# Four sequence layers on one core: three residual additions moved from VectorE to TensorE and ScalarE, new instruction orders, and a set-up that loads on two queues

## What is computed

```python
def attention_layer(x):                 # L0 and L3: linear attention, L1: softmax attention with 16 heads
    xn = layernorm(x) * w + b
    q, k, v = xn @ Wq + bq, xn @ Wk + bk, (xn @ Wv + bv) * mask
    y = attention(q, k, v)              # L0, L3: softmax of q and of k, then y = q (k^T v)
    h = layernorm(y) * (1 + scale(cond)) + shift(cond)
    return x + silu(h) @ Wout + bout    # the residual addition

def state_space_layer(x):               # L2
    s = modulated(layernorm(x)); u = layernorm(s)
    z1, z2 = (scan of width 16 over the 256 rows, forwards and backwards, for 512 channels each)
    return x + gate * ((silu(mx) * (z1 + z2)) @ Wf + bf + s)

x = L0(x); x = L1(x); x = L2(x); x = L3(x)
```

## Time and profile before

| | us |
|---|---|
| median of 3 runs | 4430.05 (4429.83 to 4433.16) |
| the profiled execution | 4430.37 |
| its span, first to last instruction | 4428.6 |
| from the start to the first scan product on POOL | 302.6 |
| from there to the last one's end | 4068 |
| from there to the last instruction | 57 |

### The profile page before, as it was taken

How to read it: one execution, slowest core, us unless ns; L and a number is a source line. 1 busy time by engine, 2 the same in 40 slices (tenths; PEclk the granted TensorE clock), 3 DMA queues, 4 the chain that set the end, 5 groups by cost and what they waited for, 6 DMA issues and landing times.

```text
span 4428.6 us, 74058 instructions
## 1 busy us (share of the span) xinstructions
PE 3722.4 (84%) x26464; PEld 2478.3 (56%) x26464; DVE 4050.2 (91%) x5619; ACT 3609.1 (81%) x8678; POOL 3849.4 (87%) x1772
## 2 busy tenths in 40 slices
PE   5988888889888888888888888888888888888664
PEld 3665555556565555555555555555655555556432
DVE  4449999989999999999999999999999999999995
ACT  0368878878988899889888998898888988988763
POOL 0019988989999999999999999999999999999994
PEclk6899999989999999999999999999999999999876
DMA  4033444543444445434444444344444444444541
GB/s 122 11 75 91 94 105 95 118 113 82 117 117 114 109 113 120 111 91 112 117 117 112 110 117 117 91 106 117 117 114 107 117 117 103 94 117 114 123 107 32
DMA packets 334160, 462.12 MB, mean 104 GB/s; under 512 B 56204, under 2 KB 165847, under 8 KB 333789
## 3 DMA queue, kind: packets, MB, share of 16 engines
q1 hardware_dynamic: 333632, 457.32, 43.7%
q10 hardware_dynamic: 158, 0.08, 0.0%
HBM read 370.26 MB, written 86.50 MB: 103 GB/s over the span
## 4 chain that ended last, share of the span: by engine, by line
ACT 28%; DVE 18%; PE 18%; POOL 7%; issue 5%; DMA 2%; SPq 0%; POOLq 0%; ACTq 0%; DVEq 0%
ACT ps L706 11%; PE ps L171 10%; DVE ps L721 5%; POOL S_X L767 5%; ACT A_ring L472 3%; DVE A_sm L429 3%; DVE S_X L721 3%; PE ps L804 3%; DVE S_X L736 2%; POOL S_X L780 2%; PE ps L376 2%; ACT C_xh L154 1%; PE ps L545 1%; ACT T_v L303 1%; DVE C_dd L579 1%
## 5 line engine op out<-in xcount | busy, mean ns | idle before, releaser
L767 POOL TENSOR_TENSOR S_X<-S_slot,S_bc 128x1024 f32<-128x1024 f32 x1024 | 2403.2, 2366 | 174.8 <-PE ps L804 119.2
L706 ACT ACTIVATE ps<-S_slot,acol 128x256 f32<-128x256 f32 x4096 | 1742.7, 468 | 190.5 <-DVE S_X L736 180.8
L721 DVE TENSOR_TENSOR_SCAN ps<-ps,S_X 128x512 f32<-128x512 f32 x1088 | 1300.0, 1214 | 37.4 <-POOL S_X L767 19.6
L780 POOL TENSOR_TENSOR S_X<-S_X,S_bc 128x1024 f32<-128x1024 f32 x480 | 1132.6, 2366 | 38.7 <-DVE S_X L721 32.6
L721 DVE TENSOR_TENSOR_SCAN S_X<-ps,S_X 128x512 f32<-128x512 f32 x960 | 1141.2, 1208 | 16.3 <-ACT ps L706 13.7
L736 DVE TENSOR_TENSOR S_X<-ps,S_bc 128x512 f32<-128x512 f32 x1088 | 712.5, 675 | 5.7 <-issue 0.2
L804 PE MATMUL ps<-S_X,sum 128*32 128x256 f32 x8192 | 615.6, 403 | 102.6 <-POOL S_X L780 62.4
L804 PEld LDWEIGHTS ps<-S_X,sum 128*32 128x32 f32 x8192 | 198.9, 112 | 388.8 <-issue 169.2
L429 DVE TENSOR_REDUCE A_sm<-ps 128x4 f32<-128x1024 f32 x256 | 311.0, 1215 | 62.7 <-PE ps L376 59.5
L376 PE MATMUL ps<-A_kP,A_qP 32*128 32x256 f32 x2048 | 292.7, 403 | 45.5 <-DVE A_sm L429 31.4
L395 PE MATMUL ps<-A_qP,A_kP 32*128 32x256 f32 x2048 | 296.7, 407 | 21.6 <-ACT A_ring L472 15.2
(11 more groups left out here) (295 smaller groups left out, 6882.0 us busy)
## 6 DMA issues: line engine op xcount, KB each, us to landing
S_slot<-scr_dd SPq DMA_DIRECT2D x1024, 256.0 KB, 4.7
scr_dd<-C_dd SPq DMA_DIRECT2D x64, 1024.0 KB, 5.3
S_bc<-scr_bc SPq DMA_DIRECT2D x256, 256.0 KB, 6.3
L_xin<-in_x SPq DMA_DIRECT2D x32, 256.0 KB
scr_x<-A_x SPq DMA_DIRECT2D x32, 256.0 KB, 5.8
T_x<-scr_x SPq DMA_DIRECT2D x32, 256.0 KB
out_x<-xs SPq DMA_DIRECT2D x32, 256.0 KB, 6.1
T_gate<-scr_gate SPq DMA_DIRECT2D x32, 128.0 KB
```

What stands on the lines that cost most here:

```text
L706: ins = a.activation(B["bank"][half_at(b, u, i)][:, n * T:(n + 1) * T], B["slot"][:, s, j, 0, :], ACT.Exp, scale=K.k["acol"][:, s, LINES * ...
L721: v.tensor_tensor_scan(line(x if u in ON_POOL else decay), line(decay), line(x), 0.0, ALU.mult, ALU.add).then_inc(S.scan.sem, 1)
L767: g.tensor_tensor(B["X"][:, u % RING], B["slot"][:, s, :, 1, :], rep(B["bc"][:, s, q, :], 1, LINES), ALU.mult).then_inc(S.b.sem, 1)
L780: g.tensor_tensor(B["X"][:, u % RING], B["X"][:, u % RING], rep(B["bc"][:, s, NQ + q, :], 1, LINES), ALU.mult).then_inc(S.cp.sem, 1)
```

## The change

**The additions.** `dve_film` is gone. `project` takes the old x as one more product, identity times x, in float32, which adds it to h in PSUM: two more products of 128x256 for each layer and batch. A step at the end of `act_film` copies the sum from PSUM to where the new x belongs, and carries the waits that the addition had. Who waited for the addition now waits for this copy.

**Loads of L0.** The input of a batch gets a semaphore of its own (`xin`), so that VectorE starts the norm's statistics with it; the mask row and the columns `L_pc` are waited for only by TensorE ahead of its k product.

**Orders.** All strings of `FIRST` and `TURN` are new. The rounds hold the same steps, but for the three additions on VectorE and the three copies on ACT.

**Set-up.** SP no longer waits ahead of its loads. 16 of them (masks, conditions, the weights of the conditioned norms) are issued by ACT. The scaling of the projections moves from VectorE to ACT. VectorE sets `bias` and splits the mask while the loads run. The bias row's way through DRAM moves from ACT to SP, behind all of its loads. The block no longer waits for the stored `pcol` to land; the loads that need it wait. The memsets of the main block, but for `A_vA`, move ahead into the set-up, and no engine but VectorE waits at the start of the main block.

```diff
-FILM_DVE = ["ystat0", "ystat1", "ymv0", "ymv1", "x"]
-FILM_ACT = ["ynm", "yln", "yrs", "ynb0", "ynb1", "yn0", "yn1", "h0", "h1", "sig1", "sig2", "sig3"]
+FILM_DVE = ["ystat0", "ystat1", "ymv0", "ymv1"]
+FILM_ACT = ["ynm", "yln", "yrs", "ynb0", "ynb1", "yn0", "yn1", "h0", "h1", "sig1", "sig2", "sig3", "x"]
...
-def project(p, bank, xT, w, bias, ones, c):
+def project(p, bank, xT, w, bias, ones, c, ident=None, x=None):
     for t in range(TT):
-        ins = matmuls(p, bank[:, t * D:(t + 1) * D], [(xT[:, k, t * P:(t + 1) * P], w[:, k, :]) for k in range(KD)] + [(ones[:, 0:P], bias)])
+        plus = [] if x is None else [(ident[:], x[:, t, :])]
+        ins = matmuls(p, bank[:, t * D:(t + 1) * D], [(xT[:, k, t * P:(t + 1) * P], w[:, k, :]) for k in range(KD)] + [(ones[:, 0:P], bias)] + plus)
...
     p.wait_ge(S.dve.sem, S.dve.at(b, "qsub"))
+    if L == "L0":
+        p.wait_ge(K.land["a"].sem, K.land["a"].at(b))
...
-    v.tensor_tensor(flat(x_out[:]), bank["o"][:, 0:512], flat(x[:]), ALU.add).then_inc(S.dve.sem, 1)
...
+    yield
+    a.wait_ge(S.pe.sem, S.pe.at(b, "o"))
+    if L == "L0" and b >= 2:
+        a.wait_ge(K.S["C"].act.sem, K.S["C"].act.at(b - 2, "xn1"))
+        a.wait_ge(K.land["x_out"].sem, K.land["x_out"].at(b - 2))
+    a.activation(flat(x_out[:]), bank["o"][:, 0:512], ACT.Copy).then_inc(S.act.sem, 1)
...
-LOADS = {"attention": 31, "conditions": 21, "scans": 21}
+LOADS = {"attention": 31, "masks": 3, "conditions": 13, "ada": 5, "scans": 21}
...
-                q.wait_ge(vector, 12)
...
-            q.dma_start(scr["pcol"].rearrange("b p n -> p b n"), M["pcol"][:]).then_inc(stored, 16)
-            q.wait_ge(stored, 16 * 3)
+            q.dma_start(scr["pcol"].rearrange("b p n -> p b n"), M["pcol"]).then_inc(K.W.columns, 16)
+            q.wait_ge(stored, 16 * 2)
...
-    "Pool": "SSCPSSSSSSSPPPSSSCSPSPSSPSPSSSPSTSPPSSSPSASPSPSCSPSLS",
+    "Pool": "SSSSTCPPSSPSPSSPSSSPSPSSPSASPSPSSCPLSSSSPSSSPSSSCPPSS",
```

More of the change, by code:

```diff
@@ L413, in pe_softmax @@
     ins.then_inc(S.pe.sem, 1)
[L414 removed]
+    yield from pe_film(p, K, S, B["ke"], B["xT"], {n: bank[i] for n, i in BANKS[L].items()}, L, b, B["x"][:, b % 2])
 def dve_softmax(v, K, b):
@@ L1214, in _ @@
             t = InTurn(a, scalar)
-            a.preload_act_table_set(ACT_SET)
+            with nc.allow_non_contiguous_dma(reason="columns of bias vectors, once"):
+                load(a, "masks", M["mi"][:], W["mask_BxS_ik0"])
+                load(a, "masks", M["mf"][:, 1, :], W["mask_BxS_ff1"])
+                load(a, "masks", M["mf"][:, 2, :], W["mask_BxSx1_fk1"].rearrange("b t a -> b (t a)"))
+                load(a, "conditions", M["cond"][:], W["cond_2048"])
+                for L, (w, b, s, n, _) in FILM.items():
+                    load(a, "conditions", M[L + "fb"][:], cols("%s_cond_%s" % (L, b)))
+                    load(a, "conditions", M[L + "fs"][:], cols("%s_cond_%s" % (L, s)))
+                    load(a, "conditions", M[L + "ft"][:], cols("%s_cond_%s" % (L, n)))
+                for L in FILM:
+                    load(a, "conditions", M[L + "fw"][:], tiles("%s_cond_%s" % (L, FILM[L][0])))
+            a.preload_act_table_set(ACT_SET)
+            a.wait_ge(vector, mark["padded"])
+            a.wait_ge(got["attention"], 16 * LOADS["attention"])
+            for L in ATTENTION:
+                for m in "qkv":
+                    padded = L == "L1" and m != "v"
+                    for i in range(KD):
+                        dst, src = k[L + "w" + m][:, i, :], M[L + m + "raw"][:, i, :]
+                        t.count(a.activation(padded_heads(dst) if padded else dst, heads(src) if padded else src, ACT.Copy, scale=M[L + "g"][:, i:i + 1]))
+            a.wait_ge(vector, mark["mparts"])
             a.wait_ge(got["conditions"], 16 * LOADS["conditions"])
@@ new lines, in _ @@
+                        load(q, "attention", M["L1%sb" % m][:] if L == "L1" and m != "v" else M["allb"][0:1, sections[L + m]], line(a[n + 1]))
+                    load(q, "attention", k[L + "wo"][:], tiles(a[8]))
+                    load(q, "attention", M["allb"][0:1, sections[L + "o"]], line(a[9]))
+                load(q, "attention", M["allb"][0:1, sections["wf"]], line("L2_cond_bf"))
+                q.dma_start(K.xin[:], K.x_in[0].rearrange("(t p) d -> p t d", p=P)).then_inc(K.land["xin"].sem, 16)
@@ L1261, in _ @@
+                load(q, "ada", M["wada"][:], W["L2_cond_Wada"].rearrange("(m p) k -> p m k", p=P))
+                load(q, "ada", M["bada"][:], line("L2_cond_bada"))
+                load(q, "ada", M["badac"][:], cols("L2_cond_bada"))
                 for n in "gb":
-                    load("conditions", M[n + "1"][:], cols("L2_cond_norm1_" + n))
-                load("scans", M["g2"][:], cols("L2_cond_norm2_g"))
-                load("scans", M["b2row"][:], W["L2_cond_norm2_b"].partition_broadcast(P))
+                    load(q, "ada", M[n + "1"][:], cols("L2_cond_norm1_" + n))
@@ L1278, in _ @@
+                    load(q, "scans", M["dp"][:, s, :], cols("L2_cond_Dp" + m))
+                    load(q, "scans", M["al" + n][:], tiles("L2_cond_Alog" + m))
             assert asked == LOADS, asked
+            q.wait_ge(vector, mark["allb"])
+            q.dma_start(scr["bias"].rearrange("(a n) -> a n", a=1), M["allb"][:]).then_inc(round3, 16)
+            q.wait_ge(round3, 16)
+            q.dma_start(M["rowsb"][:], scr["bias"].rearrange("(a n) -> a n", n=P)).then_inc(round1, 16)
             q.wait_ge(vector, mark["mparts"])
```

278 lines of the change are left out of this document (122 added, 156 removed).

## The result

Three numbers first: the changed kernel takes 4507.4 us (median of four executions), the kernel before beside it 4431.6; the ratio is 1.016 (95% interval 1.014 to 1.018). The forecast was 4352, with a range up to 4412, and had the wrong sign. The profiled execution took 4507.9 (its span is 4506.2), so its rows hold for the median.

A forecast was written before the change was run, and what follows sets the result against it. VectorE (123.4 us of a 126.05 us round) and POOL (3.4 us below) were taken to share the bound. 4430.05 - 60 (30 rounds x 2.0) - 19 (set-up) + 1 (tail) = 4352 us, range 4322 to 4412.

The forecast's parts named there:

- Set-up: Before the first scan product: first norm 22 us earlier, 3 given back, together 19 us saved (14 to 27).
- VectorE's 1.8 us a round: Three additions leave VectorE's round, 0.6 us each; with a fifth of 1.05 us of waits, rounds 2.0 us shorter.
- the passage on TensorE: Six identity products cost TensorE 2.6 us a round, hidden by its idle time; 0.87 us more latency falls into slack.
- the bound on the new orders: All lists change; at best waits ahead of additions go (round 123.2 us), at worst new waiting equals VectorE's saving (126.05).
- One (POOL is the bound): In the rounds POOL is the real bound, so a round falls by only 0.3 us: 4403 us; chance 0.22.
- Two (the set-up gives only its earlier start): New waits eat the set-up's gain beyond the 7.5 us earlier start, leaving 4.5: 4366 us; chance 0.09.
- Three (ScalarE's order): Copies waiting in ScalarE's in-order list put off exponentials and scans; round grows by 1.5 us: 4457 us, slower; chance 0.07.
- The tail: At the end of the run, identity products at the lower clock add 1.8 us at worst; taken as +1 us.

The follow-up runs named there:

- e1_setup: The changed kernel's set-up with everything else of the kernel before, additions on VectorE in the old orders; 4401 us, round 126.0 us.
- e2_moved: As e1_setup, in the orders of before, with all three additions moved to identity products on TensorE and copies on ScalarE; 4512 us, round 129.6 us.
- e9_products: As e1_setup, with the identity products on TensorE while VectorE copies from PSUM where it added; 4482 us, round 128.6 us.
- e3_orders: The changed kernel, set-up and new orders kept, with the three additions put back on VectorE; 4577 us, round 133.2 us.
- e12_filler: As e2_moved, with four products of the identity with itself behind L1's transposes, results unused; 4477 us, round 128.2 us.
- e8_copies: As e2_moved without the identity products: residual left out, ScalarE copies the layer's output alone; 4440 us, round 126.7 us.
- f4_filler12: As e1_setup, with L0's norm, transposes and q product ahead of L1's closing norm and transposes, plus twelve unused products in TensorE's gap; 4432 us, round 127.4 us.
- e4_noident: The changed kernel without the six identity products a round: residual left out, ScalarE copies the layer's output alone; 4537 us, round 130.7 us.
- e10_l1_early: As e2_moved, with L1's identity and bias products issued right behind L1's transposes; 4455 us, round 127.3 us.
- e11_l1_early_alone: As e1_setup with L1's addition alone moved, its identity and bias products issued right behind L1's transposes; 4417 us, round 126.0 us.
- f1_after_early: The changed kernel with L1's identity and bias products right behind L1's transposes, only the first of them starting a sum; 4494 us, round 129.4 us.

## Why the prediction was wrong

**Set-up: the right way, too small.** First norm 64.8 for a forecast 66; mask product 56.7 for 59; last bias DMA issued at 52.5, where I had 63 for its end; L0's k product at 80.3 waited for no columns. The first scan product came 28.4 us earlier, not 19, and above the upper end of 27; e1_setup is 26.5 us faster for it. Most of the miss lies behind the norm: from there to the first scan product it is 209.4 us for 214.6, 5.2 shorter, where I gave 3 back. SP's last load starts 10.6 us earlier (53.81 in the earlier trace rows, 43.20 after) for the 7.5 of the earlier start. And a second queue did bring bytes earlier: I had read the full DMA engines of 30 to 40 us as the rule, but from 10 to 30 us they were not full. Before, then after, with the columns of the earlier trace rows:

```profile
10.00:20.00 10.00, 0.00 (x0) 0.00 (x0) 0.00 (x0) 0.00 (x0) 0.00 (x0) 1.00 0.86 242
20.00:30.00 10.00, 6.00 (x18) 1.94 (x19) 3.79 (x11) 0.00 (x0) 0.00 (x0) 1.00 0.84 244
```
```profile
10.00:20.00 10.00, 0.00 (x0) 0.00 (x0) 7.90 (x17) 1.08 (x1) 0.00 (x0) 1.00 1.09 357
20.00:30.00 10.00, 4.86 (x12) 1.50 (x13) 6.48 (x8) 4.81 (x13) 0.00 (x0) 1.00 1.07 335
```

**VectorE's 1.8 us a round: near as a price, wrong as a gain.** The additions went, and in e2_moved VectorE is busy 122.1 us of a round, 1.3 less than before and not 1.8, and idles 7.5. Its waits there, 1500 to 3000 us, for the earlier trace rows:

```profile
DVE A_raw L136 <- issue: 28.4, 12, 2.8
...
DVE ps L722 <- ACT ps L707: 18.4, 22, 1.1
DVE T_qm L249 <- PE ps L171: 16.0, 11, 2.9
```
The first is L1's statistics, which now wait for ScalarE's copy of L0 behind longer products (the profile books it as issue): 2.4 us a round, where the addition waited 0.8.

**The step that failed** is the passage on TensorE: the six identity products are "hidden by 13 us of TensorE's idle time", and the latency from h to the new x "is offset by nothing, but each chain has its round of slack". In the orders of before it had none. I took the 13 us of TensorE's idle time for cover; but an instruction that is waited for is not hidden by idle time elsewhere. The 2.6 us were priced right (e9_products: 128.6 for 126.0) and booked at zero. Two thirds of the answer were in the trace of before: L0's and L3's output products stand whole in the chain of waits of one round. I had read its shares by engine and the sums of waits, and not its pieces. With the 2.6 us in it and no gain, my own sum would have read 4430 + 30 x 2.6 - 19 + 1 = 4490: slower.

**The second step that failed** is the bound on the new orders, that at worst they bring as much new waiting as VectorE's work falls. With the additions on VectorE their round is 133.2 us for 126.0 (e3_orders). How the changed kernel's 107 us over e1_setup divide between the two steps depends on which is taken first: the move 111 and then the orders -5, or the orders 176 and then the move -70. So the first step is shown in the orders of before; what sets the round in the new ones stays open.

**What no step had: the clock.** In e2_moved TensorE stands idle twice behind L3's end with 0.66 us of work between, and the lower level costs 1.4 us of a round (e12_filler). The sum had no term for it, and the range no room.

**The rivals.** One (POOL is the bound): no, POOL idles 122 of 1500 us. Two (the set-up gives only its earlier start): no, e1_setup has 26.5 us. Three (ScalarE's order): its sign is there, since in e2_moved VectorE waits for exponentials 1.9 us a round (lines 722 from 707, 18.4 and 3.8 of 1500) against 0.4, and in the changed kernel as much (15.1 and 6.8), its largest wait there; but in the orders of before the copies alone cost only 0.7 (e8_copies). It named the slower side, with 0.07, and in the orders of before it is at most a small part of the cause; for the new ones no run tells. **The tail**: 6.6 us longer, where 1 was forecast; e2_moved has 302.8 for before's 302.6 and e3_orders, without the move, 308.6, so it is the orders' too.

## What to carry to other kernels

Before booking an added instruction as hidden, look whether its neighbours stand in the chain of waits of a steady round, piece by piece, and also whether something that does stands right behind it on its own engine: L1's products cost 0.9 us a round in that way. Where two layers hand one buffer back and forth, the round can be a ring whose links count nearly in full though the engines idle 2 to 13%. Put added work that needs nothing new (here identity and bias products) where the engine waits anyway. And when a hand-made order opens a gap on TensorE, look at the granted clock behind it, and then test the two apart: filling the gap won 1.4 us a round in e12_filler and nothing in f4_filler12, where the order was at fault. When a move and a new order come together, run each alone before adding up what each is worth.

## What the runs showed of the hardware

- Less work on TensorE can be slower: e4_noident has six products less a round and is 0.7% slower than the changed kernel, with 16.8 us a round at the lower level for 13.4. That the clock is the cause there is not shown; the same edit in the orders of before made the kernel faster (e8_copies, 4440 for 4512). For e2_moved it is shown: 1.06 us of useless products won 1.4 us a round.
- The granted clock fell to 0.5 for 3.4 us behind waits of TensorE of 1.02 and 1.50 us with 0.66 us of work between them (e2_moved), and held behind waits of 1.67 and 1.44 us with 1.99 us of work between them (e1_setup).
- Where a product marked as start began a second sum in a PSUM bank, in other columns, while the first sum was open, L1's x came out incomplete (e10_l1_early, e11_l1_early_alone); with only the first product of the bank marked it was complete (f1_after_early). That the second start makes the next product of the first sum overwrite what it had gathered is my reading; no run looked at the numbers.
- A product of two 128 x 128 float32 tiles took 0.245 us at the higher level (24 records, 12 products, 2.94 us), where the expectations had 0.11 to 0.13.
